# Attention of a two-layer kernel: the product with v spread over twice as many steps, with more probability buffers

## The reference, cut to what matters

```python
scores = jnp.einsum('bhqd,bhkd->bhqk', q / math.sqrt(HEAD_DIM), k)
scores = scores + attention_bias                 # (8, 16, 512, 512) f32
scores = jnp.where(src_mask, -jnp.inf, scores)
probs = softmax(scores)
ctx = jnp.einsum('bhqk,bhkd->bhqd', probs, v)
x = x + (ctx.transpose(0, 2, 1, 3).reshape(B, S, D) @ Wo + bo)
h = _ln(x) * g2 + beta2
ff = _gelu2(h @ W1 + b1) @ W2 + b2
```

## Time and profile before

| | us |
|---|---|
| time, median of 3 | 1087.95 (1084.76 to 1089.02) |
| time of the profiled execution | 1084.52 |
| its span, first to last instruction | 1082.7 |
| PE / DVE / ACT / POOL busy in the span | 1017.5 / 841.2 / 797.5 / 630.1 |
| attention at its full pace | about 403 to 846 |

### The profile page before, as it was taken

One profiled execution on the slowest core, in us unless ns is written; L12 is line 12 of the kernel. 1 busy time (PEld: TensorE's weight loads), 2 busy tenths in 40 slices (PEclk: granted clock), 3 DMA queues, 4 the chain that ended last, 5 costly groups with the idle time before them and its releaser, 6 DMA issues.

```text
span 1082.7 us, 19380 instructions
## 1 busy us (share of the span) xinstructions
PE 1017.5 (94%) x6862; PEld 757.9 (70%) x6936; DVE 841.2 (78%) x1950; ACT 797.5 (74%) x1291; POOL 630.1 (58%) x317
## 2 busy tenths in 40 slices
PE   5999999998799889999999999999999899999998
PEld 4878988887565555555656556565655589999997
DVE  5599999998768788888889888888888665555553
ACT  6755567654699789999999999999989544444443
POOL 3566767673247687789877787769778142222110
PEclk9999999999899999999999999999999989999999
DMA  7746788759799998999899989999895131111001
GB/s 237 266 147 234 247 282 279 283 210 384 297 347 400 343 362 322 364 347 325 330 331 349 325 295 342 340 342 344 298 320 208 39 117 60 59 60 39 21 20 39
DMA packets 102897, 269.44 MB, mean 249 GB/s; under 512 B 7426, under 2 KB 63490, under 8 KB 86290
## 3 DMA queue, kind: packets, MB, share of 16 engines
q1 hardware_dynamic: 102802, 268.21, 69.0%
HBM read 217.57 MB, written 50.61 MB: 248 GB/s over the span
## 4 chain that ended last, share of the span: by engine, by line
PE 54%; ACT 17%; DVE 10%; DMA 7%; issue 6%; POOL 4%; SPq 2%; DVEq 0%; ACTq 0%; POOLq 0%
PE psH L537 11%; PE psT L647 10%; PE psO L537 9%; ACT t_bt L891 8%; PE psV L660 7%; PE psS L636 5%; PE psQ L537 5%; ACT t_pt L777 5%; DMA t_bt<-in_fside_Bx16xSxS 4%; POOL t_bt L1423 3%; DVE t_x L1023 2%; SPq L256 2%; PE psA L537 2%; PE psS L634 2%; PE psX L689 1%
## 5 line engine op out<-in xcount | busy, mean ns | idle before, releaser
L1423 POOL TENSOR_TENSOR t_bt<-t_bt,t_mb 128x1024 f32<-128x1024 f32 x182 | 384.5, 2149 | 115.1 <-DMA t_bt<-in_fside_Bx16xSxS 115.0
L1210 DVE CUSTOM_DVE_ANT_0 t_bt<-psS,t_bt 128x512 f32<-128x512 f32 x512 | 339.6, 687 | 87.1 <-PE psS L636 63.4
L891 ACT ACTIVATE t_bt<-t_bt,t_nm 128x512 f32<-128x512 f32 x512 | 352.6, 721 | 24.9 <-DVE t_nm L1210 24.6
L647 PE MATMUL psT<-t_idf,t_bt 128*128 128x128 f32 x2048 | 310.8, 275 | 15.5 <-ACT t_bt L891 10.7
L647 PEld LDWEIGHTS psT<-t_idf,t_bt 128*128 128x128 f32 x2048 | 250.0, 141 | 84.3 <-ACT t_bt L891 32.2
L777 ACT ACTIVATE t_pt<-psT 128x512 f32<-128x512 f32 x317 | 188.6, 595 | 31.7 <-PE psT L647 29.0
L636 PE MATMUL psS<-t_ks,t_qs 128*128 128x512 bf16 x466 | 178.3, 383 | 14.3 <-DVE t_nm L1210 11.9
L660 PE MATMUL psV<-t_pt,t_vs 128*17 128x512 f32 x1024 | 134.2, 598 | 1.0 <-ACT t_pt L777 0.9
L1220 DVE COPY t_pt<-psT 128x512 f32<-128x512 f32 x195 | 133.8, 686 | 1.4 <-PE psT L647 1.4
L636 PEld LDWEIGHTS psS<-t_ks,t_qs 128*128 128x128 bf16 x512 | 49.9, 97 | 97.0 <-DVE t_nm L1210 81.9
L1357 POOL TENSOR_SCALAR t_crs<-t_cmv 128x4 f32<-128x4 f32 x8 | 4.2, 519 | 143.2 <-DVE t_cmv L1015 143.2
(11 more groups left out here) (170 smaller groups left out, 2040.7 us busy)
## 6 DMA issues: line engine op xcount, KB each, us to landing
t_bt<-in_fside_Bx16xSxS SPq DMA_DIRECT2D x128, 1024.0 KB, 7.1
sc_qk<-t_parts SPq DMA_DIRECT2D x32, 768.0 KB, 6.6
t_qs<-sc_qk SPq DMA_DIRECT2D x16, 1024.0 KB, 9.6
t_ks<-sc_qk SPq DMA_DIRECT2D x16, 1024.0 KB, 12.1
t_wo_f<-in_L_cond_Wo SPq DMA_DIRECT2D x8, 1024.0 KB, 7.6
sc_qk<-t_parts SPq DMA_DIRECT2D x16, 512.0 KB, 7.4
t_wi_f<-in_L_cond_Wi SPq DMA_DIRECT2D x7, 1024.0 KB, 5.1
sc_v<-t_v SPq DMA_DIRECT2D x8, 544.0 KB, 7.6
```

What stands on the lines that cost most here:

```text
L647: ins = e.transpose(psT[turned_bank(n)][:, kk, :], bt[u % NB][:, t, kk * 128:(kk + 1) * 128], idf[:, :])
L891: e.activation(p, p, ACT.Exp, bias=nm[:, n % 16:n % 16 + 1], scale=-1.0).then_inc(a_exp, 1)
L1210: e.tensor_tensor_reduce(bt[u % NB][:, t, :], s, bt[u % NB][:, t, :], -1.0, 3.0e38, ALU.add, ALU.min, nm[:, n % 16:n % 16 + 1]).then_inc(v ...
L1423: e.tensor_tensor(bt[u % NB][:, hs, :], bt[u % NB][:, hs, :], mb[b % 2][:, hs, :], ALU.add).then_inc(g_M, 1)
```

## The change

Four things at once. The blocks of the product stand four tiles apart instead of two (`PSTEP`), so at 16g + 21, 25, 29, 33, and `turn_c_out` at 16g + 35; `divide` moves with them by six steps, from step 13 to step 19 of the next sequence, while the store stays at step 25 (`SLAG` 12 becomes 6). There are eight probability buffers instead of six. Room comes from one mask buffer and one result buffer instead of two, denominators kept inside `cr`, and from `wf`, cut to 2 KB a partition: each of the nine pieces is now a DMA of its own. Piece j is loaded at step 100 + 10 j and split at 109 + 10 j, and the load of piece j waits for POOL's split of piece j-1 (`g_cw`). The third stage's buffers are laid out anew, and its first input (`load_ctx(0)`, `load_x2(0)`) is brought at step N-7 instead of 384, behind a wait for transposes.

```diff
-NB, NP, NS, EARLY, MORE = 5, 6, 3, 5, 21
+NB, NP, NS, EARLY, MORE = 5, 8, 3, 5, 21
-LAG, XLAG, PSTEP, CLAG, SLAG, FIRST = 4, 1, 2, 2, 12, 20
+LAG, XLAG, PSTEP, CLAG, SLAG, FIRST = 4, 1, 4, 2, 6, 20
...
-            den = sbuf(st, "den", [128, NT, H])
+            den = cr[:, :, :, HD]
-            cx = [sbuf(st, f"cx{i}", [128, NT, D]) for i in range(2)]
+            cx = sbuf(st, "cx", [128, NT, D])
-            wf = sbuf(st, "wf", [128, NK * I])
+            wf = sbuf(st, "wf", [128, 512])
...
             for c in range(k * wd // 512):
+                load_w_at[at] = split_w_at[at + 9] = (w, c)
                 at += 10
-                split_w_at[at] = (w, c)
-            at += 16
...
             def load_mask(b):
-                if b > 1:
-                    P.wait_ge(a_mb, NT * (b - 1))
-                load(d_m[b % 2], mk[b % 2][:, :, :], mask[b])
+                P.wait_ge(a_mb, NT * b)
+                load(d_m[b % 2], mk[:, :, :], mask[b])
...
                 if n in load_w_at:
-                    w = load_w_at[n]
-                    a, k, wd = ws[w]
-                    P.wait_ge(g_cw, w_chunks[w])
-                    load(d_cw, wf[:, 0:k * wd].rearrange("p (k n) -> p k n", n=wd), kpn(a))
+                    w, c = load_w_at[n]
+                    a, _, wd = ws[w]
+                    P.wait_ge(g_cw, w_chunks[w] + c)
+                    if wd > 512:
+                        load(d_cw, wf[:, :], kpn(a)[:, c * 512 // wd, c * 512 % wd:c * 512 % wd + 512])
+                    else:
+                        load(d_cw, wf[:, :].rearrange("p (k n) -> p k n", n=wd), kpn(a)[:, c * 512 // wd:(c + 1) * 512 // wd, :])
...
-                if n == 3 * N // 4:
-                    P.wait_ge(g_cw, 9)
+                if n == N - 7:
+                    P.wait_ge(p_T, N - 12)
                     load_ctx(0)
                     load_x2(0)
...
             def split_w(w, c):
                 cs = slice(c * 512, (c + 1) * 512)
-                P.wait_ge(d_cw, 16 * ("o12".index(w) + 1))
-                copy(wl[w][0].rearrange("p k n -> p (k n)")[:, cs], wf[:, cs], a_cw)
+                P.wait_ge(d_cw, 16 * (w_chunks[w] + c + 1))
+                copy(wl[w][0].rearrange("p k n -> p (k n)")[:, cs], wf[:, :], a_cw)
...
             def divide(b):
                 P.wait_ge(v_nd, b + 1)
-                P.wait_ge(d_o[b % 2], 16 * (b // 2))
+                P.wait_ge(d_o[(b - 1) % 2], 16 * ((b + 1) // 2))
```

More of the change, by code:

```diff
@@ L38 @@
 SIDE_A, SIDE_C = (1, 3), (1, 2, 3)
-CLEAR = 28000
 PI = 3.1415925
@@ L200, in program @@
             qs, ks = [sbuf(st, "qs0", [KR, 8, S], BF16)], [sbuf(st, "ks0", [KR, 8, S], BF16)]
-            mk, mb = [sbuf(st, "mk0", [128, NT, S], U8)], [sbuf(st, "mb0", [128, NT, S], BF16)]
+            mk, mb = sbuf(st, "mk", [128, NT, S], U8), [sbuf(st, "mb0", [128, NT, S], BF16)]
             vs = [sbuf(st, "vs0", [128, NT, H, VW])]
@@ L208, in program @@
             ks.append(sbuf(st, "ks1", [KR, 8, S], BF16))
-            mk.append(sbuf(st, "mk1", [128, NT, S], U8))
             mb.append(sbuf(st, "mb1", [128, NT, S], BF16))
             vs.append(sbuf(st, "vs1", [128, NT, H, VW]))
-            den = sbuf(st, "den", [128, NT, H])
             cv = sbuf(st, "cv", [128, 512])
             cr = sbuf(st, "cr", [128, NT, H, VW])
-            cx = [sbuf(st, f"cx{i}", [128, NT, D]) for i in range(2)]
+            den = cr[:, :, :, HD]
+            cx = sbuf(st, "cx", [128, NT, D])
             ws = {"o": (Wo, NK, D), "1": (W1, NK, I), "2": (W2, NM, D)}
@@ L230, in program @@
             chf = [sbuf(st, f"chf{i}", [128, S]) for i in range(3)]
-            fT = [sbuf(st, f"chT{n}", [128, NM, S], F32R) for n in "hl"]
+            fT = [sbuf(st, "chTh", [128, NM, S], F32R)]
             x3 = [sbuf(st, f"x3{i}", [128, NT, D]) for i in range(2)]
-            hl = [sbuf(st, f"hl{i}", [128, NT, D]) for i in range(2)]
+            os_ = [sbuf(st, "os0", [128, NT, D])]
             warm = sbuf(st, "warm", [128, NM])
             cstt, cmv, crs = sbuf(st, "cstt", [128, NT, 6]), sbuf(st, "cmv", [128, NT, 2]), sbuf(st, "crs", [128, NT])
-            os_ = [sbuf(st, f"os{i}", [128, NT, D]) for i in range(2)]
-            sbuf(st, "clear", [128, CLEAR])
+            sbuf(st, "clear", [128, 16])
             ccs.insert(0, sbuf(st, "cin0", [128, NT, D]))
             cxs.insert(0, sbuf(st, "rin0", [128, NT, D]))
+            fT.append(sbuf(st, "chTl", [128, NM, S], F32R))
+            hl = [sbuf(st, f"hl{i}", [128, NT, D]) for i in range(2)]
+            os_.append(sbuf(st, "os1", [128, NT, D]))
         w_chunks, load_w_at, split_w_at, at = {}, {}, {}, 100
@@ L244, in program @@
             w_chunks[w] = len(split_w_at)
-            load_w_at[at] = w
             for c in range(k * wd // 512):
+                load_w_at[at] = split_w_at[at + 9] = (w, c)
                 at += 10
-                split_w_at[at] = (w, c)
-            at += 16
         def sync_program(e):
@@ L461, in attention_loads @@
                     P.wait_ge(g_n, b + 1)
-                    load(d_o[b % 2], sc_c[b], cx[b % 2][:, :, :])
+                    load(d_o[b % 2], sc_c[b], cx[:, :, :])
             def load_ctx(b):
@@ L912, in read_mask @@
                     P.wait_ge(g_M, masks(16 * (b - 1) - 2, 1))
-                e.activation(mb[b % 2][:, t, :], mk[b % 2][:, t, :], ACT.Copy, scale=NEG).then_inc(a_mb, 1)
+                e.activation(mb[b % 2][:, t, :], mk[:, t, :], ACT.Copy, scale=NEG).then_inc(a_mb, 1)
             def split_w(w, c):
                 cs = slice(c * 512, (c + 1) * 512)
-                P.wait_ge(d_cw, 16 * ("o12".index(w) + 1))
-                copy(wl[w][0].rearrange("p k n -> p (k n)")[:, cs], wf[:, cs], a_cw)
+                P.wait_ge(d_cw, 16 * (w_chunks[w] + c + 1))
+                copy(wl[w][0].rearrange("p k n -> p (k n)")[:, cs], wf[:, :], a_cw)
             def attention(n):
@@ L1230, in context_out @@
                     P.wait_ge(v_na, b + 1)
-                    P.wait_ge(v_ch, chain(e.tensor_tensor(den[:, :, :], cr[:, :, :, HD], nb, ALU.mult)))
-                    P.wait_ge(v_ch, chain(e.reciprocal(den[:, :, :], den[:, :, :])))
-                    e.tensor_tensor(den[:, :, :], den[:, :, :], nb, ALU.mult).then_inc(v_nd, 1)
+                    P.wait_ge(v_ch, chain(e.tensor_tensor(den, cr[:, :, :, HD], nb, ALU.mult)))
+                    P.wait_ge(v_ch, chain(e.reciprocal(den, den)))
+                    e.tensor_tensor(den, den, nb, ALU.mult).then_inc(v_nd, 1)
             def attention(n):
@@ L1427, in split_w @@
                 P.wait_ge(a_cw, w_chunks[w] + c + 1)
-                low(wl[w][1].rearrange("p k n -> p (k n)")[:, cs], wf[:, cs], wl[w][0].rearrange("p k n -> p (k n)")[:, cs], g_cw)
+                low(wl[w][1].rearrange("p k n -> p (k n)")[:, cs], wf[:, :], wl[w][0].rearrange("p k n -> p (k n)")[:, cs], g_cw)
             def divide(b):
                 P.wait_ge(v_nd, b + 1)
-                P.wait_ge(d_o[b % 2], 16 * (b // 2))
-                e.tensor_tensor(cx[b % 2][:, :, :].rearrange("p t (h d) -> p t h d", d=HD), cr[:, :, :, 0:HD],
-                                den[:, :, :].unsqueeze(3).broadcast_to([128, NT, H, HD]), ALU.mult).then_inc(g_n, 1)
+                P.wait_ge(d_o[(b - 1) % 2], 16 * ((b + 1) // 2))
+                e.tensor_tensor(cx[:, :, :].rearrange("p t (h d) -> p t h d", d=HD), cr[:, :, :, 0:HD],
+                                den.unsqueeze(3).broadcast_to([128, NT, H, HD]), ALU.mult).then_inc(g_n, 1)
             def attention(n):
```

## The result

The changed kernel takes 1098.12 us (1093.02 to 1102.53, six executions) against 1085.49 for the kernel before in the same rounds; the ratio is 1.0113, 95% interval 1.0080 to 1.0145. It is slower, by 12.6 us at the medians. The prediction said 1086, range 1073 to 1098, so the time lies just above the range, on the side that I gave 0.21.

The account below looks back on a forecast made before the run. No engine alone was taken to bound attention: PE and ACT alternate twice a group, transfers near the path. Terms -10.3 - 1.5 + 10.7 + 0.5 = -0.6 us against 1084.52; adjusted to the shown median, 1086 us, range 1073 to 1098.

Parts of the forecast that it names:

- the side that I gave 0.21: Whole kernel: slower than before by more than 0.5%, above 1093.4 us; chance 0.21.
- Blocks every fourth tile: Attention groups: evenly spaced blocks bring 17.13 us a group to 16.6, 1.037 a tile; -10.3 us, ends -19 and 0.
- The two-tile handover: Between last block and turn, PE has two tiles, 1.3 us, for ACT's copy; wait taken as 0.2 us a group.
- The nine pieces: Steps 100 to 192: SP waits for POOL's splits, ACT for pieces, bias comes late; +10.7 us, ends +3 and +21.
- the even pace: Blocks spread evenly over the tiles, forecast at 1.037 us a tile; as a rival with pieces' waits hidden, 1077 us, chance 0.28.
- the walk: Step-by-step times of SP's releases from step 100, bringing ACT to step 192 at +112.8 us against +102.1 before.
- Divide six steps later: POOL's mask addition goes ahead of divide and comes 1.9 us sooner; -1.5 us before step 100, ends 0 and -1.9.
- my four cases: Own sum 0.45; even spacing wins 0.28; slower rounds of pieces 0.14; no gain from spreading 0.13.
- One of my signs of being wrong: Late stretch: tiles stay at 1.07 us each, with DVE idle for POOL.
- The third stage's first input: Load near step N - 8 costs nothing; after the last score ACT's copy nears PE's turn: +0.5 us, ends 0 and 1.1.
- pieces' rounds decide: Steps 110 to 180: SP's wait for `g_cw` outweighs the gain, 17 to 24 us, 1099 at 3 us a piece; chance 0.14.
- the spreading brings nothing: Attention: bias transfers carry the pace once PE doesn't, leaving +10.7 us less 3, 1094 us; chance 0.13.

Follow-up runs that it names:

- run 8: The kernel before without the two multiplications of the denominators by the mask flag: 1081.72 us, ratio 0.9969.
- run 5: The changed kernel with pieces 40 tiles apart, each split 19 steps after its load, and without the two mask-flag multiplications: 1070.20 us, ratio 0.9899.
- run 4: The changed kernel without the two multiplications of the denominators by the mask flag: 1081.66 us, ratio 0.9972.
- run 7: The changed kernel without the two mask-flag multiplications, pieces 20 tiles apart, each split 19 steps after its load: 1074.41 us, ratio 0.9910.
- run 9: The changed kernel without the two mask-flag multiplications, pieces 40 tiles apart, each split 5 steps after its load: 1083.21 us, ratio 0.9998.
- run 6: The changed kernel with pieces 40 tiles apart, split 19 steps after load, and both mask-flag multiplications on POOL ahead of divide: 1070.46 us, ratio 0.9899.
- run 2: The kernel before with only the end of a group (turn, copy, denominators, divide) moved six steps later: 1093.20 us, ratio 1.0077.

## Why the prediction was wrong, by its own steps

Three terms make the result: the even spacing, with the eight buffers and the rest of the change that was not tried apart, run 8 to run 5, 1070.2 - 1081.7 = -11.5 us; the pieces at ten tiles, run 5 to run 4, 1081.7 - 1070.2 = +11.5; the multiplications on POOL's additions, +16.5 in the changed kernel (run 4) against the 2.7 that they cost before (run 8), +13.8. Sum +13.8, measured +12.6. The first two rest on run 5 and share its 5.6 us to either side.

The profiled executions show where on the way the time went. Tiles are counted from 0 by DVE's bias additions (L1210 before, L1211 after), and each stretch is the time between two of their starts; the forecast is the prediction's own term for the stretch:

| | forecast, us | before, us | changed, us | difference |
|---|---|---|---|---|
| start to tile 100 | -1.5 | 403.2 | 402.1 | -1.2 |
| tile 100 to 192, the pieces | +10.7 | 100.1 | 109.7 | +9.6 |
| tile 192 to 511, the late stretch | -10.3 | 342.5 | 341.7 | -0.8 |
| tile 511 to the end | +0.5 | 236.9 | 237.7 | +0.8 |

Only the late stretch is off. In run 4, which has no multiplications, its 319 tiles take 327.9 us, and in run 8 339.9. So in these executions, one of each kernel, the spacing gains 12.0 us there, and the multiplications take 13.8 (341.7 - 327.9).

*Blocks every fourth tile: right.* I forecast -10.3 for the late stretch, at 1.037 a tile. Without the multiplications on either side it is -12.0, at 1.028. The two-tile handover was sized well: PE waits for ACT's copy 5.2 us in run 5's 32 groups, 0.16 a group where I took 0.2. In the changed kernel's late stretch blocks stand 4.14 us apart (590.14 to 602.56 in three intervals), inside the 3.7 to 4.3 that I named.

*The nine pieces: right in mechanism and nearly in size.* I forecast +10.7 for steps 100 to 192, the even pace included; the table has +9.6 by DVE's tiles, and run 4 against run 8 has +12.2 (112.0 - 99.8). The releases of SP that I walked out, 21, 27, 44, 56, 70, 81, 92, 105 us after SP's step 100, can be read in SP's timeline of the changed kernel (step 100 at 400.99):

```profile
422.95 0.33 SPq L255 DMA_DIRECT2D t_wf<-in_L_cond_W  x1
423.33 1.38 SPq L255 DMA_DIRECT2D t_bt<-in_fside_Bx16xSxS  x3
428.36 0.33 SPq L255 DMA_DIRECT2D t_wf<-in_L_cond_W  x1
...
444.72 0.33 SPq L255 DMA_DIRECT2D t_wf<-in_L_cond_W  x1
...
455.96 0.33 SPq L255 DMA_DIRECT2D t_wf<-in_L_cond_W  x1
...
471.06 0.38 SPq L255 DMA_DIRECT2D t_wf<-in_L_cond_W  x1
...
483.03 0.38 SPq L255 DMA_DIRECT2D t_wf<-in_L_cond_W  x1
...
495.05 0.37 SPq L255 DMA_DIRECT2D t_wf<-in_L_cond_W  x1
...
507.76 0.38 SPq L255 DMA_DIRECT2D t_wf<-in_L_cond_W  x1
```

That is 22.0, 27.4, 43.7, 55.0, 70.1, 82.0, 94.1 and 106.8. ACT's exponential at step 192 starts at 513.97, 113.0 us after SP's step 100; the walk said 112.8. Three bias loads leave together behind the first, as forecast, and SP's waits for splits sum to 68.4 us in its view of waits (forecast some 70).

So close a match has some luck in it. ACT waited 9.9 us for pieces, near the four waits of 2 to 3 us that I forecast, but not where I had them: 2.35 us at step 119, 4.75 at step 149, 1.46 at step 189 and little elsewhere. The landing was mis-sized too. The 5.3 to 8.9 us of the earlier trace rows are of one 256 KB load and two of 1 MB, and the changed kernel's pieces, which go out first when the waiting queue moves on, landed sooner (nine loads of `t_wf`; the second line is of the eight pieces of W1 and W2):

```profile
DMA to landing us min/median/max: 2.5/3.6/7.5
...
t_wf<-in_L_cond_W SPq DMA_DIRECT2D x8, 256.0 KB, 3.3
```

The estimate of 2.6 us that the prediction set aside was nearer to the median, though the Trainium skill's page "DMA: Bandwidth & Descriptors" gives that fit for the path of DMAs issued by GpSimd (section "Anatomy of one DMA — SWDGE (gpsimd) path"), and these are issued by SP.

What I did not separate is who hurts: SP's wait alone costs about 4 us (run 7, not clear of noise), and run 9 shows that some 9 us of ACT's waiting cost 10.5 us in span and 13 at the median. Whether the two add in the changed kernel was not isolated.

*Divide six steps later, and the denominators at no cost: here it failed.* I moved `divide` past the queue of POOL and priced that, and priced `turn_c_out` and the copy by their handover. But `context_out` carries the three small operations of the denominators along with it to step 19, and I gave them no cost because the row of before has 0.27 and 0.23 us. That duration holds for a place where POOL stands idle. At step 19 POOL adds the mask of the unit that came late behind q and k. DVE waits up to 1.7 us in the first multiplication and 1.2 in the second, with tile 20's score queued behind it. None of my four cases had it, so the other terms, each near what the stretches show, came to -0.6 instead of +12.6. Run 4 takes the operations out and gains 16.5 us, run 6 has POOL do them and keeps that gain, and run 2 moves the end of a group alone and loses 8.2. Why the same move costs 8.2 us on the kernel before and 13.8 with the even spacing stays open; with the even spacing the late stretch leaves PE 1.2% idle (run 5), with the old one 4.4%, so there is less spare time to hide a stall in.

One of my signs of being wrong came half true: the late stretch stayed at 1.07 us a tile, but its DVE row names no idle time for POOL among the largest. The wait stands inside the multiplications' own durations, where a column of idle time does not show it.

*The third stage's first input*, the buffers and the 1.5 us of `divide`: the first and last rows of the table are near their terms; none was tried apart.

The rival "pieces' rounds decide" had the right sign, and its 1099 us lies close to the measured time, but that is luck: the pieces cost 11.5 to 13.7 us, not the 17 to 24 that it needed. The rival "the spreading brings nothing" matches what the late stretch looks like, 312 tiles in 334 us, and is wrong about why; only with the multiplications taken out do the gain and the loss separate.

## What to carry to other kernels

When a step moves in a hand-written order, list every instruction that moves with it and look at what the *other* engines do at the new place; a duration from the old trace belongs to its old neighbours. On DVE a small operation with two SBUF inputs should not stand where POOL works through long ones: here half a microsecond of work a sequence cost 16.5 us over eight sequences, and the same work on POOL cost nothing that could be measured. Such a wait is seen in the spread of an operation's durations (272/1287/2018 ns) and not in idle time. A buffer cut so far that each load waits for the use of the one before puts a round trip into the queue of all loads; with room between the same pieces, run 5's trace has no wait of SP for a split or of ACT for a piece. An unchanged pace in a stretch can be a gain and a loss of the same size.

## What the runs showed of the hardware that was not expected

PE's stalls can cost twice. At 446.67 a bias load was issued behind q and k and took 12.81 us to land; POOL added the mask to it from 459.55. Until 459.0 PE was at work (8.80 of the 10 us from 450 to 460), then it had nothing to do for 3.63 us; ACT waited 4.75 us in the same stretch for a piece. At about 461.9 the granted clock fell, and it stayed at the lower of its two levels, 1.2 instead of 2.4 GHz, until about 468.6. The timeline of PE, two windows and the chain there:

```profile
458.44 0.60 PE L648 MATMUL psT<-t_idf,t_bt 128*128 128x128 f32 x4 [0.16 <-issue]
462.67 0.61 PE L637 MATMUL psS<-t_ks,t_qs 128*128 128x512 bf16 x1 [3.63 <-DVE t_nm L1211]
```

```profile
461.00:462.00 1.00, 0.00 (x0) 0.00 (x0) 0.09 (x1) 0.00 (x0) 1.00 (x2) 0.96 1.05 395
462.00:468.00 6.00, 5.33 (x23) 2.89 (x23) 5.04 (x14) 5.15 (x9) 6.00 (x4) 0.50 0.90 366
```

```profile
463.27 0.85 PE psT L648 x4
464.13 0.43 PE psS L637
...
466.86 1.84 PE psV L661 x8
468.70 0.36 PE psS L637
469.06 0.44 PE psT L648 x4
```

Four transposes take 0.85 instead of 0.44 and a block 1.84 instead of 0.98, until 468.7. PE worked for some 6 us at half speed, so about 3 us are lost in this one place on top of the stall (an estimate from these rows). A second place is at 427 to 431 us, where the mean granted clock is 0.60. In run 2 the denominators themselves do it: after their stall at 455.05 to 458.72 PE had no work for 2.07 us, and the clock was 0.50 from 460 to 463. Over 380 to 846 us the mean granted clock was 1.00 before, 0.99 in the changed kernel, 0.98 in run 2 and 1.00 in run 5. So a part of what the waits cost comes through the clock; no run separates it. The prediction had no such term.

The executions of the changed kernel also spread more: 1093.0 to 1102.5 with mean granted clocks of 0.978 to 0.985, where the kernel before stays within 5.2 us in each set of its executions. Run 4 has clocks as different (0.979 to 0.986) and lies between 1080.1 and 1083.4, and runs 5 and 6 each had one of four executions near 1080. How much of the spread is the clock stays open.
